# Scratch image and output of a two-layer image kernel: partition p holds image rows 2p and 2p+1 instead of rows p and p+128

## What is computed

```python
# layer 0: shifts, channel mixing and a gate, on the group-normalised image
x = x + _L0_conv_ref(_gn(x), ...)       # per batch a softmax of two branches, 64x64 channel mixing, sigmoid gate
# layer 1: Fourier layer on the group-normalised result
x_ft = jnp.fft.rfft2(_gn(x))
top  = jnp.einsum('bixy,ioxy->boxy', x_ft[:, :, :32, :32], w1)
bot  = jnp.einsum('bixy,ioxy->boxy', x_ft[:, :, -32:, :32], w2)
x = x + jnp.fft.irfft2(out_ft with top and bot set, s=(256, 256))
```

## Time and profile before

| | us |
|---|---|
| median of 3 runs | 2876.54 (2876.23 to 2878.68) |
| the profiled execution, device time | 2875.03 |
| its span, first to last instruction | 2873.3 |

### The profile page before, as it was taken

How to read it: one execution, slowest core, us unless ns; L and a number is a source line. 1 busy time by engine, 2 the same in 40 slices (tenths; PEclk the granted TensorE clock), 3 DMA queues, 4 the chain that set the end, 5 groups by cost and what they waited for, 6 DMA issues and landing times. The chain is left out here.

```text
span 2873.3 us, 38693 instructions
## 1 busy us (share of the span) xinstructions
PE 2230.3 (78%) x15026; PEld 1350.6 (47%) x15026; DVE 1704.3 (59%) x1705; ACT 1317.1 (46%) x1541; POOL 576.0 (20%) x411
## 2 busy tenths in 40 slices
PE   0000169999999999979999999927676989899784
PEld 0000023333333333329999999926663444445342
DVE  8999769999999999972333333310002445455442
ACT  1111158888898988856555455400002222221220
POOL 1000034543355555620000000000000111111112
PEclk9999989999999999989999999969888999999887
DMA  9999479999999999978777677579998999999999
GB/s 401 431 431 422 193 223 344 346 338 340 347 342 346 348 345 341 349 232 332 259 257 260 254 257 259 185 249 363 379 388 285 412 407 402 407 388 413 405 380 394
DMA packets 470460, 966.45 MB, mean 336 GB/s; under 512 B 14417, under 2 KB 391809, under 8 KB 424993
## 3 DMA queue, kind: packets, MB, share of 16 engines
q1 hardware_dynamic: 264784, 636.45, 59.7%
q10 hardware_dynamic: 169984, 192.95, 19.9%
q0 software_dynamic: 35536, 134.84, 12.0%
HBM read 670.59 MB, written 293.60 MB: 336 GB/s over the span
## 5 line engine op out<-in xcount | busy, mean ns | idle before, releaser
L610 PE MATMUL psum<-mix_u,wcur 128*64 128x512 f32 x2048 | 882.7, 593 | 24.5 <-DVE mix_u L690 24.5
L610 PE MATMUL psum<-mix_v,wcur 128*64 128x512 f32 x2048 | 882.7, 593 | 0.0
L610 PEld LDWEIGHTS psum<-mix_u,wcur 128*64 128x64 f32 x2048 | 278.4, 136 | 613.5 <-issue 605.0
L1171 PE MATMUL psum<-tab_irow_icol_sign,inv_t 128*128 128x512 f32 x1024 | 494.0, 606 | 10.8 <-DVE weights_or_rows L1266 10.2
L1266 DVE TENSOR_TENSOR weights_or_rows<-weights_or_rows,psum 128x1024 f32<-128x1024 f32 x224 | 272.9, 1221 | 256.6 <-PE psum L1171 232.0
L587 POOL COPY mix_v<-mix_u 64x2321 f32<-64x2321 f32 x128 | 375.2, 2931 | 10.4 <-PE psum L610 2.3
L1002 DVE COPY fwd_cols<-psum 128x544 f32<-128x544 f32 x128 | 141.9, 1108 | 394.0 <-PE psum L796 394.0
L796 PE MATMUL psum<-tab_frow_fcol_both_ident,fwd_x 128*128 128x128 f32 x3072 | 351.4, 276 | 2.4 <-DMA fwd_x<-x_scratch 2.4
L796 PEld LDWEIGHTS psum<-tab_frow_fcol_both_ident,fwd_x 128*128 128x128 f32 x3072 | 347.5, 193 | 3.7 <-DMA fwd_x<-x_scratch 2.5
L702 DVE SCALAR_TENSOR_TENSOR gated<-psum,pcur,gated 128x2048 f32<-128x2048 f32 x128 | 300.5, 2348 | 41.6 <-PE psum L610 41.3
L709 DVE SCALAR_TENSOR_TENSOR gated<-gated,centred 128x2048 f32<-128x2048 f32 x128 | 316.8, 2475 | 4.0
(11 more groups left out here) (184 smaller groups left out, 1654.6 us busy)
## 6 DMA issues: line engine op xcount, KB each, us to landing
mix_u<-x SPq DMA_DIRECT2D x120, 1280.0 KB, 9.3
stat_x<-x SPq DMA_DIRECT2D x64, 2048.0 KB, 12.4
x_scratch<-gated ACTq DMA_DIRECT2D x128, 1024.0 KB, 8.9
weights_or_rows<-x_scratch SPq DMA_DIRECT2D x112, 1024.0 KB, 10.5
out<-weights_or_rows POOLq DMA_DIRECT2D x112, 1024.0 KB, 15.3
fwd_x<-x_scratch SPq DMA_DIRECT2D x96, 1024.0 KB, 6.8
x_tile<-x_scratch SPq DMA_DIRECT2D x46, 1024.0 KB, 9.3
weights_or_rows<-L_conv_w_real SPq DMA_DIRECT2D x8, 4096.0 KB, 31.3
```

The costliest lines, as they stand in the source:

```text
L610: last = nc.tensor.matmul(bank(k * 4 + q, 512, C, e * C), wcur[j][:, e, m * C:(m + 1) * C], taps[e][:, r0:r0 + 2, m:m + W], start=(m == 0) ...
L1171: last = nc.tensor.matmul(bank(n % 2 * 2 + a), TS[n % 2][:, a * P:(a + 1) * P], icol, start=True, stop=True)
```

## The change

Partition p takes rows 2p and 2p+1 of the image wherever rows lie on partitions.

- The scratch image is laid out (pair, 128 row pairs, batch in pair, channel, 2 rows, column). A mixing tile's store is 4 runs of 2 KB for each partition, still one DMA of 1 MB.
- A forward or inverse tile is loaded with one DMA of 2 MB, one run of 16 KB for each partition; the partitions lie 256 KB apart in the scratch image (128 KB before).
- An output tile is stored with one DMA of 2 MB, 8 runs of 2 KB for each partition.
- Tiles are held (channel, 2 rows, column); the tables `frow` and `irow` follow the new order of rows. ACT's square reads a contiguous run; DVE's add reads PSUM in another order.
- Semaphore counts go by 16 a tile instead of 32, and SP's loop over pairs of batches in the inverse stage is written out.

```diff
-        a = th * np.outer(np.arange(P) + half * P, np.arange(NM))
+        a = th * np.outer(2 * np.arange(P) + half, np.arange(NM))
...
-        x1 = nc.dram_tensor("x1_scratch", (NQ, H, 2, C, W), F32, kind="Internal").ap()
+        x1 = nc.dram_tensor("x1_scratch", (NQ, P, 2, C, 2, W), F32, kind="Internal").ap()
...
-        x1_rows = x1.rearrange("q h e c w -> h q e (c w)")
-        out_rows = out.rearrange("b c h w -> h (b c) w")
+        x1_rows = x1.rearrange("q h e c a w -> h q e (c a w)")
+        out_rows = out.rearrange("b c (h a) w -> h (b c) (a w)", a=2)
...
-                        act.dma_start(x1_out[q:q + 1, :, y0:y0 + SP_, :].rearrange("b p r w -> (b p) r w"),
-                                      G[n % 4][:, :].rearrange("p (r w) -> p r w", w=W)).then_inc(stored[n % 4], 16)
+                        act.dma_start(x1_out[q, :, y0 // 2:(y0 + SP_) // 2, :],
+                                      G[n % 4][:, :].rearrange("p (h k) -> p h k", k=2 * W)).then_inc(stored[n % 4], 16)
...
-                        for a in (1, 0):
-                            sp.dma_start(XW[t % NX][:, a, :, :].rearrange("p c w -> p (c w)"),
-                                         x1_rows[a * P:(a + 1) * P, c // 2, c % 2, g * W:(g + CG) * W]
-                                         ).then_inc(loaded[t % NX], 16)
+                        sp.dma_start(XW[t % NX][:, :, :, :].rearrange("p c a w -> p (c a w)"),
+                                     x1_rows[:, c // 2, c % 2, g * 2 * W:(g + CG) * 2 * W]).then_inc(loaded[t % NX], 16)
...
-                    body(0, True)
-                    with sp.Fori(1, B // 2) as i:
-                        body(i, False)
+                    for i in range(B // 2):
+                        body(i, i == 0)
...
-                            xw = XW[G0 % NX][:, :, 2 * cp:2 * cp + 2, :].rearrange("p a c w -> p a (c w)")
+                            xw = XW[G0 % NX][:, 2 * cp:2 * cp + 2, :, :]
...
                             nc.vector.tensor_tensor(xw, xw, psum[:, n % 2 * 1024:n % 2 * 1024 + 1024]
-                                                    .rearrange("p (a k) -> p a k", a=2), ALU.add).then_inc(added, 1)
+                                                    .rearrange("p (a c w) -> p c a w", a=2, c=2), ALU.add).then_inc(added, 1)
...
-                                for a in range(2):
-                                    pool.dma_start(out_rows[a * P:(a + 1) * P,
-                                                            bass.ds(batch(i, G0 // NG) * C + group_at(G0), CG), :],
-                                                   XW[G0 % NX][:, a, :, :]).then_inc(stored[G0 % NX], 16)
+                                pool.dma_start(out_rows[:, bass.ds(batch(i, G0 // NG) * C + group_at(G0), CG), :],
+                                               XW[G0 % NX][:, :, :, :].rearrange("p c a w -> p c (a w)")
+                                               ).then_inc(stored[G0 % NX], 16)
```

More of the change, by code:

```diff
@@ L102, in constants @@
     kx = np.concatenate([np.arange(M1), np.arange(-M1, 0)])
-    ar = th * np.outer(kx, row)
+    ar = th * np.outer(kx, row.reshape(P, 2).T.reshape(-1))
     put("irow", np.concatenate([np.cos(ar), -np.sin(ar)], 0))
@@ L528, in program @@
             SHIFT = PITCH + 1
-            x1_out = x1.rearrange("q h e c w -> q (e c) h w")
+            x1_out = x1.rearrange("q h e c a w -> q (e c) h (a w)")
             def rows_of(t):
@@ L718, in program @@
         KEPT = 1
-        x1_kept = [sb(top, f"x1_tile{i}", [P, 2, CG, W]) for i in range(KEPT)]
+        x1_kept = [sb(top, f"x1_tile{i}", [P, CG, 2, W]) for i in range(KEPT)]
         ph = ExitStack()
@@ L726, in program @@
             NX = 4
-            XW = [sb(ph, f"fwd_x{i}", [P, 2, CG, W]) for i in range(NX - KEPT)] + x1_kept
+            XW = [sb(ph, f"fwd_x{i}", [P, CG, 2, W]) for i in range(NX - KEPT)] + x1_kept
             A = [sb(ph, f"fwd_cols{i}", [P, 2, 4 * NP, C]) for i in range(2)]
             XB = sb(ph, "fwd_modes", [C, 3, KX, M2])
-            junk = [sb(ph, f"fwd_junk{i}", [P, 2, 2 * W]) for i in range(2)]
+            junk = [sb(ph, f"fwd_junk{i}", [P, 4 * W]) for i in range(2)]
             part = [sb(ph, f"fwd_part{i}", [P, C // 2]) for i in range(2)]
@@ L752, in loaded_by @@
             def loaded_by(t):
-                return (t // NX + 1) * 32
+                return (t // NX + 1) * 16
             with nc.Block() as block:
@@ L881, in squares @@
                                 act.wait_ge(sq_done, k - 1)
-                            nc.scalar.activation(junk[g % 2][:, :, :],
-                                                 XW[t % NX][:, :, 2 * g:2 * g + 2, :].rearrange("p a c w -> p a (c w)"),
+                            nc.scalar.activation(junk[g % 2][:, :],
+                                                 XW[t % NX][:, 2 * g:2 * g + 2, :, :].rearrange("p c a w -> p (c a w)"),
                                                  ACT.Square,
@@ L1088, in x_load @@
                         c0 = group_at(g)
-                        for a in (1, 0):
-                            sp.dma_start(XW[g % NX][:, a, :, :].rearrange("p c w -> p (c w)"),
-                                         x1_rows[a * P:(a + 1) * P, bass.ds(i * -1 + (NQ - 1), 1), 1 - j,
-                                                 c0 * W:(c0 + CG) * W].rearrange("p b k -> p (b k)")
-                                         ).then_inc(loaded[g % NX], 16)
+                        sp.dma_start(XW[g % NX][:, :, :, :].rearrange("p c a w -> p (c a w)"),
+                                     x1_rows[:, NQ - 1 - i, 1 - j, c0 * 2 * W:(c0 + CG) * 2 * W]).then_inc(loaded[g % NX], 16)
                     for g in range(KEPT):
-                        sp.sem_inc(loaded[g], 32)
+                        sp.sem_inc(loaded[g], 16)
                     sp.wait_ge(mixed, 2 * 2 * NCH + 2)
@@ L1261, in _ @@
                             G0, cp = n // 4, n % 4
-                            xw = XW[G0 % NX][:, :, 2 * cp:2 * cp + 2, :].rearrange("p a c w -> p a (c w)")
+                            xw = XW[G0 % NX][:, 2 * cp:2 * cp + 2, :, :]
                             if cp == 0:
-                                dve.wait_ge(loaded[G0 % NX], i * (2 * NG // NX * 32) + G0 // NX * 32 + 32)
+                                dve.wait_ge(loaded[G0 % NX], i * (2 * NG // NX * 16) + G0 // NX * 16 + 16)
                             dve.wait_ge(col_done, i * (2 * NR) + 2 + n + 1)
                             nc.vector.tensor_tensor(xw, xw, psum[:, n % 2 * 1024:n % 2 * 1024 + 1024]
-                                                    .rearrange("p (a k) -> p a k", a=2), ALU.add).then_inc(added, 1)
+                                                    .rearrange("p (a c w) -> p c a w", a=2, c=2), ALU.add).then_inc(added, 1)
                 @block.gpsimd
```

10 lines of the change are left out of this document (5 added, 5 removed).

## The result

The changed kernel is slower than the kernel before, by a ratio of 1.0018, 95% interval 1.0011 to 1.0025: 2884.71 us median (2876.73 to 2889.01, 20 runs) beside 2878.66 us (2873.67 to 2882.65, 20 runs). Run a second time, in a session of its own, it came out at 1.0009 (1.0000 to 1.0019), so the loss is small and known only roughly. The forecast was 4.9 us less. The middle of the interval is 5.2 us more, on the other side of no change.

The account below looks back on a forecast made before the run. Mixing and forward were taken as bound by PE, the inverse stage by the DMA engines. Gains of 2 + 2.6 + 0.3 = 4.9 us off 2875.03 gave 2870.1, or 2871.6 for the median; range 2858 to 2883.

Parts of the forecast that it names:

- The bound: Inverse stage: the DMA engines limit from 2217.61 us on; 30 us of room before PE's own end at 2830 us.
- The scratch loads: Scratch image loads as one DMA with 16 KB runs: 4.87 us a tile instead of 4.91, 2 us gained on 56 tiles.
- DVE's waits for tiles: Inverse stage: DVE's waits for loads, 7 times and 24.6 us together before the change, were to be shorter.
- Rival D: Inverse stage: 16 KB load packets hold up 4 KB store packets, stream runs thin; up to 62 us slower, 2938; chance 0.04.
- The output stores: Output stores with 2 KB runs and one semaphore write: 0.04 us a tile, 2.6 us gained; ends nothing and 4.2 us.
- The last mixing store: End of mixing: only the last 1 MB store is on the path, 2.7 us instead of 3.0, 0.3 us gained.
- Mixing: Mixing's stores with 2 KB runs take DMA time off a stage where PE has no gap: nothing, same length to 1 us.
- Forward: Forward stage: one load DMA instead of two, 4.9 us of PE's 8.5 a tile: nothing, same length to 1 us.
- DVE's add, POOL's issues, ACT, SP: Instructions of the changed tiles: add's scattered PSUM read, one store issue, ACT's square, SP's unrolled loop: no cost or gain.
- B: Output stores: a packet holds four runs and grows to 8 KB; 19 us gained in all, 2857; chance 0.03.
- C: Output stores: POOL's 2 KB runs no longer joined into packets; 15 to 24 us more, 2889 to 2898; chance 0.05.
- E: Scratch loads: doubled distance between partitions slows them; inverse stage pays 62 us, 2938, at 348 GB/s; chance 0.01.

## Why the prediction was wrong

**The bound: right.** The inverse stage is set by the DMA engines and all else runs at PE's pace. In the version with two loads and without pause the last add came at 2832 us, 2 us from the forecast's 2830. Two parts of that bound were not seen: the pause, 7.1 us of the stage in the kernel before, and the mode loads at 213 to 217 GB/s.

**The scratch loads: wrong in sign, and the step that failed.** "Gain 0.04 us a tile, on 56 tiles: 2 us" took the rate of a shape that runs alone and applied it to a shape that runs beside another queue. Alone the gain is nil (428 against 427). In company it is a loss of 7.6 us beside the single store DMA, by single profiles 4.7 from the packet's length and 2.9 from one DMA standing for two. DVE's waits for tiles, which were to be shorter, rose from 24.6 to 40.3 us (42.3 in the second profile). "All rates are read where one shape runs alone" is the sentence to take back.

**Rival D named the right place and had too small a chance.** "Loads in 16 KB packets hold up the 4 KB store packets beside them": the packet counts show just that. I dismissed it for the joint rate of 418 GB/s, which is indeed hardly moved (417 after). That number could not speak for or against it: the sum of two queues stays the same while their shares go from 2:1 to 4:1. The price was not a load at 348 GB/s, 62 us: a 16 KB packet takes 611 ns in the median of the stage, and 611 alone (2196 to 2204 us). Against the kernel before it was a lower rate in the first 320 us, in part engines without a packet. How the turns of the packets bring that about is not shown.

**The output stores: the term was too small.** The bound of "at most 2.0 ns a packet" by the straight line was broken: 416 GB/s against 405, and stores 5.02 us apart (2859.66 to 2864.68 us) instead of 5.17, 0.15 us a tile where I had allowed 0.065. Two DMAs with 2 KB runs have it too (2860.26 to 2865.27 us), and two with 1 KB runs in the new layout are back at 5.17 (2844.81 to 2849.97), so it comes from the runs. In the stage it showed as 1.2 us for the runs and 4.2 for one DMA instead of two, 5.4 in all against 2.6 and an upper end of 4.2. The new layout with loads and stores as before costs 1.2 us of it again (672.0 against 670.8), for which the forecast had nothing; both 1.2 are within what two profiles differ by.

**The last mixing store, 0.3 us:** too small to be seen.

**Mixing and "as long as before to 1 us": wrong by 2 us.** "Takes DMA time off a stage in which PE has no gap: nothing" looked at the total and not at who waits for whom: the loads that feed PE share the engines with the stores, and longer store packets take more of them.

**Forward: right to about 1 us.** Once PE runs at 2.4 GHz, 512 of its matmuls by `frow` take 72.9 us in both traces. Its first matmuls (L796 before, L794 now) start at 1295.5 us before and 1298.7 after, and the windows of the granted clock, kernel before and then changed kernel, tell why the changed kernel takes a microsecond more:

```profile
1295.00:1299.00 4.00, 3.50 (x18) 3.51 (x18) 0.00 (x0) 3.53 (x7) 0.00 (x0) 0.54 1.01 426
1299.00:1304.00 5.00, 5.00 (x47) 5.00 (x46) 1.12 (x1) 4.36 (x9) 0.00 (x0) 1.00 1.02 429
```

```profile
1295.00:1299.00 4.00, 0.49 (x2) 0.41 (x3) 1.23 (x6) 0.30 (x1) 0.00 (x0) 0.50 1.00 426
1299.00:1304.00 5.00, 5.00 (x25) 5.00 (x26) 0.00 (x0) 4.40 (x9) 0.00 (x0) 0.51 1.03 439
```

In both the clock has fallen to half (1.2 GHz) in a wait of 14 us for a table; it is back at 1299 us before and only about 1304 after, so that 5 us of matmuls instead of 3 run at the low level. From first to last of these matmuls the stage takes 569.1 to 569.5 us in the five profiles with 1 KB mixing stores and 569.4 to 570.7 in the other fourteen, so this microsecond goes with the mixing store; why was not looked into.

**DVE's add, POOL's issues, ACT, SP: right,** no cost. **Rivals B, C, E: right to be small.** Packets stayed at 4 KB, the stores alone got faster, and loads with partitions 256 KB apart run at 428 GB/s.

**The sum** by the measured terms: +7.6 for the loads, -5.4 for the stores and +1.2 for the layout make the stage's +3.4; with +2 for mixing and +1 for the low clock it is +6.4 us. The result's interval is 3.2 to 7.2 us. That the sum lies in it is no proof of each term, for most are differences of two profiles.

## What to carry to other kernels

Where two DMA queues share the engines, look at the bytes of a packet on either side: packets are served in turn, so a longer run gives its own queue more of the bytes at the cost of the other, even if neither runs faster alone. Ask which queue is waited for; here it was the stores', and loads cut to the stores' 4 KB gave 0.9946. Look also for the point at which a loop waits for the last of its transfers: leaving out that pause gave 0.9978 in the kernel before with one edit, as much as the new layout with two loads and the pause kept (0.9977). And a mean DMA share of 1.00 can hide microseconds in which nothing moves.

## What the runs showed of the hardware

- 16 KB, 8 KB, 4 KB and 2 KB load packets were each served one for one with the 4 KB store packets, where both queues had work (101 to 101, 383 to 381, 554 to 550, 282 to 281). The run with eight loads of 2 KB, 2555 to 2559 us, where the loads get less than a third of the bytes:

```profile
q0 software_dynamic: 281, 1.15, 69.8%
q1 hardware_dynamic: 282, 0.52, 33.6%
```

- A longer window can mislead: from 2551 to 2561 us the same run counts 864 load packets to 631, for from 2553 to 2555 us, after one store ended, few store packets were under way (311 to 79).
- The mode loads, 8 KB runs over 64 partitions, moved at 217 GB/s alone at a full DMA share, the tiles' loads over 128 partitions at 427 and 428.
- 2 KB load packets alone made 406 GB/s.
- POOL's stores with 2 KB runs travel in packets of the same 4 KB as those with 1 KB runs and are 2.7% faster alone (416 against 405 GB/s).
- A 128-element copy on DVE took 2.15 us instead of 0.24 while POOL copied 2321 elements for each of 64 partitions. Of the eight such copies in each trace, the two before and three after that ran beside this copy of POOL's took 2.14 to 2.15 us, the others 0.20 to 0.25.
